# A graph-layer kernel: x read a second time in turned blocks, and the first gathers let go before the product is finished

## The reference, cut to what matters

```python
# x: 8192 x 512 f32; src, dst: 131072 edges; weight W: 512 x 512
h    = einsum('nf,ef->ne', layernorm(x), W)
x    = x + segment_sum(edge_weight[:, None] * h[dst], src, 8192)
# then a small seven-layer network on a few columns of layernorm(x) changes
# 32 columns, and x = x + (that result)
x    = x + ffn(layernorm(x)[None], ffn_W, ffn_b)[0]
```

## Time and profile before

| | |
|---|---|
| median of 3 runs | 1710.06 us (1707.35 to 1710.17) |
| the profiled execution's own time | 1711.71 us |
| its span, first to last instruction | 1709.9 us |
| PE busy | 1573.4 us (92%) |
| DVE busy | 1111.9 us (65%) |
| ACT busy | 587.8 us (34%) |
| POOL busy | 1076.6 us (63%) |
| granted TensorE clock | 0.992 |
| DMA | 323.82 MB, mean 189 GB/s |

### The profile page before, as it was taken

The page is one execution under the profiler, slowest core; times in us unless marked ns, Lnnn a source line. Parts: engine busy times, 40 slices in busy tenths (PEclk is TensorE's granted clock), DMA queues, the critical chain, the costliest instruction groups (busy, mean ns, idle before and its releaser), DMA issues.

```text
span 1709.9 us, 28124 instructions
## 1 busy us (share of the span) xinstructions
PE 1573.4 (92%) x3952; PEld 642.9 (38%) x3953; DVE 1111.9 (65%) x4099; ACT 587.8 (34%) x1287; POOL 1076.6 (63%) x1099
## 2 busy tenths in 40 slices
PE   7999998999999999999999999999999999999996
PEld 4555553333333333333333333333333333333442
DVE  7666683767677786767776867777753333336794
ACT  6777732222222222222221222222224444444332
POOL 2000003777777777777777777777777777777870
PEclk9999999999999999999999999999999999999998
DMA  7333224777777777677767677776777777777563
GB/s 249 130 136 122 106 72 128 215 204 201 203 202 205 203 204 205 200 202 207 203 199 207 194 205 202 201 202 197 202 205 210 209 210 210 210 209 203 176 219 112
DMA packets 130733, 323.82 MB, mean 189 GB/s; under 512 B 29410, under 2 KB 48130, under 8 KB 130562
## 3 DMA queue, kind: packets, MB, share of 16 engines
q0 software_dynamic: 81920, 268.50, 54.8%
q1 hardware_dynamic: 48642, 53.48, 9.3%
HBM read 288.36 MB, written 33.55 MB: 188 GB/s over the span
## 4 chain that ended last, share of the span: by engine, by line
PE 69%; DVE 16%; issue 7%; DVEq 3%; DMA 3%; ACT 0%; POOL 0%; SPq 0%; POOLq 0%; ACTq 0%
PE psum L1330 51%; PE psum L1196 12%; DVE region L936 4%; DVE region L845 3%; DMA region<-h_rows,region 2%; DVEq L936 2%; DVE region L831 2%; PE psum L1185 2%; PE psum L1362 2%; DVE region L837 2%; DVE region L1016 1%; DVE region L839 1%; DVE region L843 1%; PE psum L1206 1%; DVE region L1077 1%
## 5 line engine op out<-in xcount | busy, mean ns | idle before, releaser
L551 POOL DMA_INDIRECT region<-h_rows,region x1024 | 1013.5, 990 | 580.5 <-DMA h_rows<-region 268.7
L1330 PE MATMUL psum<-region 128*128 x2552 | 1206.5, 611 | 106.1 <-DVE region L936 53.5
L1330 PEld LDWEIGHTS psum<-region 128*128 128x128 f32 x2552 | 440.5, 189 | 828.2 <-issue 818.7
L936 DVE SCALAR_TENSOR_TENSOR region<-region 128x128 f32 (+1 forms) x1276 | 444.7, 351 | 368.3 <-PE psum L1330 246.3
L712 ACT ACTIVATE x<-psum 128x512 f32<-128x512 f32 x192 | 114.7, 597 | 771.6 <-PE psum L1330 771.6
L1196 PE MATMUL psum<-region 128*128 128x512 f32 x512 | 230.2, 593 | 0.8 <-ACT region L610 0.8
L845 DVE COPY_PREDICATED region<-region 128x256 f32<-128x256 int32 x407 | 179.1, 440 | 0.0
L691 ACT ACTIVATE psum<-x 128x512 f32<-128x512 f32 x256 | 153.7, 601 | 8.1
L831 DVE TENSOR_TENSOR region<-region 128x128 int32<-128x128 f32 x452 | 128.7, 285 | 24.9 <-ACT region L637 23.4
L843 DVE TENSOR_TENSOR region<-region 128x128 f32<-128x128 f32 x452 | 128.2, 284 | 0.0
L839 DVE TENSOR_TENSOR region<-region 128x128 f32<-128x128 f32 x452 | 127.7, 283 | 0.1
(11 more groups left out here) (146 smaller groups left out, 590.1 us busy)
## 6 DMA issues: line engine op xcount, KB each, us to landing
x<-in_x SPq DMA_DIRECT2D x16, 1024.0 KB, 5.5
h_rows<-region SPq DMA_DIRECT2D x64, 256.0 KB, 2.0
region<-h_rows,region POOLq DMA_INDIRECT x1024, 3.7
out<-x SPq DMA_DIRECT2D x4, 2816.0 KB, 10.3
out<-x SPq DMA_DIRECT2D x4, 1024.0 KB, 12.5
region<-in_L_gnn_weight SPq DMA_DIRECT2D x1, 1024.0 KB, 5.6
out<-x SPq DMA_DIRECT2D x3, 256.0 KB, 3.0
region<-in_src SPq DMA_DIRECT2D x4, 128.0 KB, 3.0
```

The lines of the kernel that those rows point to most:

```text
L551: pool.indirect_dma_start(gathered[:, (c + 1) % RING, :], None, h_dram, bass.IndirectOffsetOnAxis(ap=dst_i[g][:, i:i + 1], axis=0),).then_ ...
L936: dve.scalar_tensor_tensor(spread[:, slot % SR, :], iota_n[:, bass.ds((tile - (g * T + 1)) * P, P)], src_f[g][:, bass.ds(chunk - (g * NC + ...
L1330: pe.matmul(banks[:, bass.ds(pe.snap(tile_wanted) % AGG, 1), :].rearrange("p t f -> p (t f)"), spread[:, slot % SR, :], gathered[:, bass.d ...
```

## The change

1. The host also passes x in turned blocks, `x_blocks`, the same 16.8 MB in another order. SP loads them two tiles at a time into eight slots (`load_pair`). `turn_x` and `xT_out` are gone.
2. ACT does four units of statistics a tile, not three, and ten before the first tile.
3. DVE and PE find the largest row that part 0 reads (`far`). POOL starts the gathers of part 0 once part 0 has its indices, all statistics of x are done, and the h rows up to `far` are stored.
4. The gathers of part 0 have a ring of WIDE = 42 slots: tiles 32 to 63 of `x1` and the old ten. The old ten lie on the product's buffers, so gather 31 waits for the last matmul of the product (`s_mm`). POOL now also waits for the landing of the gather ten before.
5. Tiles 32 to 63 of x are therefore not in SBUF during part 0. Their seeds are loaded from DRAM by ACT, three ahead (`load_seed`), their sums are stored to the DRAM tensor `summed_rows` (`put_by`), and in part 1 loaded from there again.
6. `plan()` assumes 3.43 us a tile, not 3.86. The sort of each part now has to be finished 40 steps before the walk of the part before it ends (LAST_STEPS), not 12, and the slots are spread over each part by itself.
7. DVE's builds wait for the last matmul alone; its wait for the h stores stands at step 8, and the large memset moves into the last part. The small network's weights are loaded from chunk 320 on, not 16. Each second tile from 25 to 43, SP copies rows of x into two tiles of `h_rows` that are not yet written.

```diff
@@ sync @@
+            def load_pair(b):
+                if b >= XS // 2:
+                    sp.wait_ge(s_mm, 2 * b - XS + 2)
+                elif 2 * b >= XS - KD:
+                    sp.wait_ge(s_wtr, KD)
+                j = b % (XS // 2)
+                sp.dma_start(xT[:, 2 * j:2 * j + 2, :, :].rearrange("p s k n -> p s (k n)"),
+                             x_blocks[2 * b:2 * b + 2, :, :].rearrange("t p f -> p t f")).then_inc(s_xt[j], 16)
...
+                if n % 2:
+                    if n // 2 + XS // 2 < T // 2:
+                        load_pair(n // 2 + XS // 2)
+                    late = next(to_fill, None) if n >= 2 * (LOADS - FIRST_LOADS) else None
+                    if late is not None:
+                        sp.dma_start(h_dram[late * P:(late + 2) * P, :], x[late * P:(late + 2) * P, :]).then_inc(s_fill, 16)
+                    continue
@@ gpsimd @@
-            for u in range(4):
-                pool.wait_ge(s_hst[u], 16 * (T // 4))
...
             for c in range(CH):
                 g, i = divmod(c, NC)
-                if c >= RING:
-                    slot_free(c - RING)
+                into, n_slots = ring_of(g)
+                at = WIDE - n_slots + (c + 1) % n_slots
+                if at in holds:
+                    slot_free(holds[at])
+                holds[at] = c
+                if c >= RING:
+                    pool.wait_ge(s_gat[c % RING], 16 * (c // RING))
                 if i == 0:
                     pool.wait_ge(s_index, g + 1)
+                if c == 0:
+                    pool.wait_ge(s_sd, LOADS)
+                    near_rows_stored()
+                if c + 1 == T - KEPT:
+                    pool.wait_ge(s_mm, T)
+                if c == NC:
+                    for u in range(4):
+                        pool.wait_ge(s_hst[u], 16 * (T // 4))
@@ scalar @@
+            def load_seed(k):
+                g, n = divmod(k, OUTSIDE)
+                if g > STAGED_PARTS:
+                    return
+                mine = slice(n * P, (n + 1) * P)
+                if g:
+                    stored = k - OUTSIDE
+                    act.wait_ge(s_summed[stored % OUTS], 16 * (stored // OUTS + 1))
+                act.dma_start(seed_in[:, k % SEEDS, :], summed_dram[mine, :] if g else x[KEPT * P:, :][mine, :]
+                              ).then_inc(s_seed_in[k % SEEDS], 16)
...
+            def put_by(u):
+                k = outside(u)
+                if k is not None and u // T < STAGED_PARTS:
+                    n = k % OUTSIDE
+                    act.wait_ge(s_agg, u + 1)
+                    act.dma_start(summed_dram[n * P:(n + 1) * P, :], summed_out[:, k % OUTS, :]
+                                  ).then_inc(s_summed[k % OUTS], 16)
@@ vector @@
             dve.wait_ge(s_mm, T)
-            for u in range(4):
-                dve.wait_ge(s_hst[u], 16 * (T // 4))
@@ tensor @@
-            turn_x(0)
-            turn_x(1)
             turn_w()
             for n in range(T):
-                if 0 < n < T - 1:
-                    turn_x(n + 1)
                 multiply(n)
```

More of the change, by code:

```diff
@@ L13, with gnn_ffn @@
 AX_X = mybir.AxisListType.X
-def gnn_ffn(nc, x, src, dst, edge_weight, gnn_w, ffn_w, ffn_b, out):
+def gnn_ffn(nc, x, src, dst, edge_weight, gnn_w, ffn_w, ffn_b, x_blocks, out):
     P = 128
@@ L39, in gnn_ffn @@
     RING = 10
+    KEPT = 32
+    STAGED_PARTS = 1
+    WIDE = T - KEPT + RING
+    SEEDS, OUTS = 3, 3
+    XS = 8
+    FILLED = 44
     SR = 8
@@ L108, in plan @@
                         "counts": 2.0, "rows": 2.0, "index": 0.4, "source": 0.8}
-        turn, tile, start = 0.9, 3.86, 15.5
+        turn, tile, start = 0.9, 3.43, 15.5
         vector, tensor, n, behind, inverts, b = 3.0, start, 0, [], [], 0
@@ L153, in share @@
             return {"keys": 1.0, "weights": 0.9, "turned": 0.9, "flip": 0.4, "rest": 0.5}.get(what, 0.7)
[L155 to L162, removed]
+        found = [0] * (PARTS * NS)
+        for part in range(1, PARTS):
+            shares = [share(what) for g, (what, _, _) in left if g == part]
+            first, end = max(0, (part - 1) * NS - LAST_STEPS), part * NS - LAST_STEPS
+            room, at = (end - first) / sum(shares), 0.0
+            for of_one in shares:
+                found[first + int(at * room)] += 1
+                at += of_one
         return found
@@ L345, in gnn_ffn @@
         s_free = sem("slots_free")
+        s_fill = sem("late_rows_filled")
+        s_near = sem("needed_rows_stored")
+        s_seed_in = [sem(f"seed_rows_loaded{k}") for k in range(SEEDS)]
+        s_summed = [sem(f"summed_rows_stored{k}") for k in range(OUTS)]
         s_op = sem("spreads_ready")
@@ L701, in _ @@
                 seed(u)
+            for u in range(4):
+                act.wait_ge(s_hst[u], 16 * (T // 4))
+            for k in range(SEEDS):
+                load_seed(k)
             for u in range(PARTS * T):
@@ L1176, in turn_w @@
                     last.then_inc(s_wtr, 1)
[L1178 to L1186, removed]
             def multiply(n):
-                pe.wait_ge(s_tev, n + 1)
+                pe.wait_ge(s_xt[n // 2 % (XS // 2)], 16 * (n // XS + 1))
                 if n < 4:
@@ L1195, in multiply @@
                 for k in range(KD):
[L1196 removed]
+                    last = pe.matmul(bank(n % 4), xT[:, n % XS, k, :], wT[:, k, :], start=(k == 0), stop=(k == KD - 1))
                 last.then_inc(s_mm, 1)
@@ L1251, in of_sort @@
                     turned[g] += 1
+                    if g == 0 and turned[g] == FAR_BEHIND - 1:
+                        pe.wait_ge(s_far, 1)
+                        pe.transpose(bank(FAR_BANK)[0:1, 0:P], far_col[:, :], ident[:, :]).then_inc(s_far_turned, 1)
                 elif what == "maxima summed":
@@ L1349, in _ @@
             assert turned == [TURNS] * PARTS
-            rows = [slice(e * GP, (e + 1) * GP) for e in range(2)]
+            half_rows = [slice(e * GP, (e + 1) * GP) for e in range(2)]
             def halves(l):
```

173 lines of the change are left out of this document (120 added, 53 removed).

## The result

The changed kernel takes 1656.95 us (median of 4 runs, 1652.66 to 1660.23) beside 1708.7 us for the kernel before in the same comparison: a ratio of 0.970, 95% interval 0.967 to 0.972. The forecast was 1647, the range 1630 to 1676. The gain is 52 us where 63 were forecast. The profiled execution took 1660.23 us, with a span of 1658.5.

A forecast was written before the change was run, and what follows sets the result against it. The prediction took POOL's gathers to bound the walk and PE the first stage. The last gather comes 68.4 us earlier, less 5 us for transfers: 63.4 us off 1710.06 gives 1647 us, range 1630 to 1676.

The forecast's parts named there:

- The first stage: Product of x and W: PE bounds it at 3.44 us a tile, ACT needs at most 3.1, transfers stay hidden.
- H: End of the product, seen in ACT's last copy: forecast to move from 274.4 to 246.2 us.
- The early gathers: POOL's gathers 0 to 30 before the product ends: indices about 193 us, 40 us of gathers until 233, all 31 fit.
- Can the walk use the lead?: Part 0's walk up to gather 256: PE through step 309 after 290 us, POOL asking after 296, so no stall.
- outer bound: Stall at gather 256 if every DVE wait at a turn stays, 35 us: 310 us, a stall of 14.
- The lead is not usable: Rival: DVE's denser sort paces part 0 above 0.96 us a step, up to 40 us lost, 1657 to 1687; chance 0.20.
- the likeliest case: Whole kernel as forecast, 1636 to 1656 us; chance 0.58.
- main engine of the chain: Sign of a wrong forecast: DVE is the chain's main engine between the product's end and 290 us later.
- The extra transfers: Second half of part 0: seeds and sums make the DMA engines just full, 167 us in 166; 5 us taken.
- the 992 intervals: POOL's gathers 31 to 1023 after the product: 1240 us at 1.25 each, plus 47.6 us beside the sort's 328 pairs.
- the rival with late seeds: Walk's seeds, asked two tiles ahead (10.4 us), land too late; at 12 us a load 1749 us; chance 0.04.
- Parts 1 to 3: Later walk: parts 2 and 3 sorted within 319 steps, DVE needs 283 of POOL's 332 us; POOL stays the bound.

The follow-up runs named there:

- late_second: Against the changed kernel, the sort of part 2 and of part 3 begins with the walk of the part before, not 40 steps earlier; ratio 0.969, 1650.38 us.
- the three doses: Kernels with 0, 11 (the changed kernel) and 24 pairs of part 1 sorted before the product ends; ratios 0.977, 0.970 and 0.960.
- no_transfers: Against the changed kernel, seeds after the first three and all stores of sums are left out, results false; ratio 0.966, 1647.64 us.
- no_head: Against the changed kernel, no pair of part 1 is sorted before the product ends, instead of 11; ratio 0.977, 1666.21 us.
- head: Against the changed kernel, the planner's slot cost is 0.57 us, not 0.65, so 24 pairs of part 1, not 11, precede the product's end; ratio 0.960, 1637.13 us.

## Why the prediction was right

**The first stage held.** H was forecast at 246.2 and the last copy stands at 246.55. ACT did not take over: its 44.7 us in 50 are the 3.1 us of a tile's 3.44 that were worked out. The transfers were not quite for nothing (a share of 0.88 in the first window), but PE did not wait.

**The early gathers held.** Indices at 192.4 (forecast 193), gather 30 at 234.83 (233), gather 31 at 247.27 (246.4), the interval from there to gather 255 at 1.297 (forecast 296 / 225 = 1.316). The pause before H was 11.5 us, 13 forecast.

**"Can the walk use the lead?" was mis-sized.** This is the step that missed: 290 us after H for step 309, and no stall. PE began that step 308.2 us after the product (555.5 against 247.3), and the stall was 19.7 us. The mechanism, DVE's sort against a ring that shrinks to ten, was the one named as the dangerous one; its size was wrong. From PE's first step, 1.5 us after the product, two terms carried the error. The 30 steps from 279 on were put at 0.88 us, as though DVE only built; the plan starts the next part's sort exactly there, and they took 32.1 us instead of 26.4 (late_second: 25.8). The 279 steps before took 274.6 instead of 262: a few microseconds for handing over were too few, and a pair costs 1.3 us of the walk in the three doses, not 1.14. Of these 12.6 us some 3 went again in no_transfers.

The prediction's outer bound, 310 us and a stall of 14, was nearly reached, but not in the way it was worked out. It was for the case that DVE's waits at the turns stay, 35 us. Between 248 and 524 us they nearly vanished, 2.5 us in four waits, as the forecast had said for a DVE that is the slower one:

```profile
DVE rows L987 <- PE psum L1328: 2.5, 4, 0.9
```

That the number came near is luck.

**"The lead is not usable" was half true.** The forecast gave it 0.20. Its price was 40 us at most, and half of that came. The sign that the prediction set for it, a longer gap near gather 256 put down to PE's line, appeared, and 1656.95 lies 1 us outside the 1636 to 1656 of the likeliest case. The prediction also called itself wrong should DVE be the main engine of the chain in this stretch. It was not: line 1452 of PE has 61.6% of the chain between 248 and 558 us, and no line of DVE more than 6.0%. That sign was badly chosen, since the chain names PE, and yet sorting less beside the walk is what removed the wait.

**What kept the total near.** The last gather was forecast at 1539 and went out at 1549.31. The stall's 19.4 us beyond a usual interval were in part made up by two terms that were too dear: 5 us for the transfers, which POOL did not pay as a slower interval, and 1287.6 us for the 992 intervals, which took 1282.7 without the stall. The product's end adds 0.9. So the range held, in part by errors that cancel.

**The extra transfers.** The 5 us taken are near what no_transfers returned (3.6 us in its trace, some 6 in the time, with overlapping intervals), but not where they were put: POOL's interval in the second half is 1.29 us as everywhere, and it never waited for a landing. The share was 0.92, not the 1.0 or more of the sum, so here the shares of the two kinds of transfer don't simply add. The Trainium skill ("DMA: Bandwidth & Descriptors", Where 436 GB/s comes from) puts the limit by bytes, near 358 GB/s; the trace agrees in so far as 304 GB/s went through. Landings did grow, 5.0 and 5.4 us for 256 KB from and to ACT's queue against 2.0 for a store of h before, but two tiles of notice covered them, and the rival with late seeds did not appear.

**Parts 1 to 3 held.** POOL stayed the bound, 1.292 us an interval, although each sort has fewer steps.

The sum again, in the spans of the two profiled executions: 1709.9 - 28 (H) - 3 (no wait for stores) - 40 (lead) + 20 (stall) + 2 (tail) - 2 (rounding and the interval) = 1659, measured 1658.5.

## What to carry to other kernels

A head start for the engine that sets the pace is worth only what the next slower chain can follow: here 31 early gathers gave as much as 15, and a buffer that shrinks later is the place where the surplus is taken back. Before buying slots, look for an idle stretch of the engine that will limit next; DVE sat idle for 25.3 us just ahead of the walk, and sorting thirteen more pairs before it, 15 us of DVE's work, brought 16 us. And when work is planned in advance from assumed costs, set them from the trace again after each change (0.65 us assumed for a slot; a pair of two takes 1.14, so 0.57). Last, a lead of one engine pays only while that engine sets the pace: on the chip with the lower clock the kernel with the early gathers was 19 us slower than the one without.

DVE's first build after the change, with that idle time before it:

```profile
248.06 0.35 DVE L1064 SCALAR_TENSOR_TENSOR rows<-rows 128x128 f32<-128x128 int16 x1 [25.25 <-issue]
```

## What the runs showed of the hardware

**What sorting on VectorE costs the gathers beside it.** In no_head DVE is idle for 41.8 us before its first build at 246.15, and POOL's gathers there are perfectly even; three of them:

```profile
218.19 0.95 POOL L630 DMA_INDIRECT rows<-h_rows,rows  x1 [0.30 <-issue]
...
219.44 0.94 POOL L630 DMA_INDIRECT rows<-h_rows,rows  x1 [0.30 <-issue]
...
220.69 0.94 POOL L630 DMA_INDIRECT rows<-h_rows,rows  x1 [0.30 <-issue]
```

In the changed kernel the same stretch has 11 pairs of the sort beside it, and one gather takes 2.72 us (the row at 219.22 above); 30 intervals take 40.3 us instead of 38.1. In head, with more pairs beside them, 30 intervals take 42.2 us and one gather 3.93. The Trainium skill ("SBUF — State Buffer", Who interferes with whom) describes something like it: a copy in a two-port mode holds the port that GpSimd needs for descriptors. The trace agrees in the direction, and the price here is about 0.2 us a pair, with rare long ones. A pair has five instructions, one of them a copy; which of them costs POOL this no run shows.

**The chip can decide which engine is the bound.** At a mean granted clock of 0.994 POOL sets the pace, with 1.04 us a step against 0.86 for PE. On the chip with 0.918, where PE also has gaps that no semaphore explains, a step takes 1.23 us and POOL waits for PE; the same change is worth 0.8% instead of 3.0%. How much of this is the clock's and how much the gaps' was not separated.
